# Spectral mamba stage: two of sixteen channels of the scan's feed on POOL, the skip term as one product of 512 columns

## The reference, cut to what matters

```python
dA = jnp.exp(dt[..., None] * A)
dBx = dt[..., None] * Bm[:, :, None, :] * xc[..., None]
def step(h, inp):
    dA_t, dBx_t, C_t = inp
    h = dA_t * h + dBx_t
    y = jnp.einsum('bds,bs->bd', h, C_t)
    return (h, y)
...
y = ys.transpose(1, 0, 2) + xc * D
y = y * jax.nn.silu(z)
return y @ out_w.T
```

## Time and profile before

| | us |
|---|---|
| median of 3 runs | 7898.19 (7890.61 to 7903.71) |
| the profiled execution | 7902.44, span 7900.3 |
| spectral stage: first feed to end of last scan | 5623.05 to about 7652.7 in the span |

### The profile page before, as it was taken

The page is one execution under the profiler, slowest core; times in us unless marked ns, Lnnn a source line. Parts: engine busy times, 40 slices in busy tenths (PEclk is TensorE's granted clock), DMA queues, the critical chain, the costliest instruction groups (busy, mean ns, idle before and its releaser), DMA issues. The chain is left out here.

```text
span 7900.3 us, 122279 instructions
## 1 busy us (share of the span) xinstructions
PE 6835.9 (87%) x38266; PEld 3658.0 (46%) x38266; DVE 5843.1 (74%) x5708; ACT 4011.5 (51%) x6797; POOL 3601.8 (46%) x2430
## 2 busy tenths in 40 slices
PE   8967699999965499778999999999899999999970
PEld 7842333333244145662222222222477777777750
DVE  4652577777613385018999999999799999999975
ACT  4423366666612474015666666666455555555532
POOL 0100122222202000006777777777687787787860
PEclk9988799999977798668999999999899999999985
DMA  2252234334357333440000000000000000000016
GB/s 70 69 174 103 58 99 99 99 99 100 92 124 236 129 101 116 120 65 14 14 14 14 13 15 13 13 15 9 15 11 10 10 10 11 9 10 10 10 40 188
DMA packets 560486, 478.16 MB, mean 61 GB/s; under 512 B 181789, under 2 KB 486851, under 8 KB 551771
## 3 DMA queue, kind: packets, MB, share of 16 engines
q1 hardware_dynamic: 560155, 473.52, 21.9%
HBM read 306.97 MB, written 163.76 MB: 60 GB/s over the span
## 5 line engine op out<-in xcount | busy, mean ns | idle before, releaser
L2657 POOL TENSOR_TENSOR spe_hc<-spe_hs,spe_cu 128x1024 f32<-128x1024 f32 x552 | 1291.3, 2359 | 312.0 <-DVE spe_hs L2854 312.0
L2253 POOL TENSOR_TENSOR spa_hc<-spa_hs,spa_cr 128x966 f32<-128x966 f32 x592 | 1224.2, 2068 | 426.5 <-DVE spa_hs L2527 410.4
L2527 DVE TENSOR_TENSOR_SCAN spa_hs<-spa_p_d,spa_hs,spa_bx 128x483 f32<-128x483 f32 x1168 | 1359.4, 1204 | 0.0
L2854 DVE TENSOR_TENSOR_SCAN spe_hs<-spe_p_d,spe_bx 128x1024 f32<-128x1024 f32 x552 | 1233.8, 2275 | 106.3 <-ACT spe_p_d L2803 105.6
L2731 PE MATMUL spe_p_y<-spe_idt,spe_hc 128*128 128x128 f32 x8832 | 1039.7, 276 | 0.0
L2731 PEld LDWEIGHTS spe_p_y<-spe_idt,spe_hc 128*128 128x128 f32 x8832 | 1018.1, 193 | 0.0
L1048 DVE TENSOR_REDUCE attention_nm<-attention_p_s 128x2 f32<-128x640 f32 x1024 | 788.9, 812 | 259.6 <-PE attention_p_s L905 258.6
L2803 ACT ACTIVATE spe_p_d<-spe_p_d 128x896 f32<-128x896 f32 x552 | 474.1, 900 | 918.8 <-PE spe_p_d L2716 918.4
L1006 ACT ACTIVATE attention_pr<-attention_p_t 128x512 f32<-128x512 f32 x1280 | 710.6, 599 | 421.4 <-PE attention_p_t L928 288.7
L2438 ACT ACTIVATE spa_p_d<-spa_p_d,spa_av 128x483 f32<-128x483 f32 x1184 | 704.0, 634 | 410.7 <-PE spa_p_d L2310 408.5
L2310 PE MATMUL spa_p_d<-spa_du,spa_hot 32*128 32x483 f32 x2368 | 643.1, 618 | 58.4 <-DVE spa_hs L2527 49.2
(11 more groups left out here) (417 smaller groups left out, 10585.6 us busy)
## 6 DMA issues: line engine op xcount, KB each, us to landing
attention_qs<-scratch_qp SPq DMA_DIRECT2D x768, 64.0 KB, 2.8
attention_rc<-scratch_den SPq DMA_DIRECT2D x128, 256.0 KB
scratch_qp<-patch_parts SPq DMA_DIRECT2D x96, 256.0 KB, 2.0
spa_xt<-scratch_x SPq DMA_DIRECT2D x148, 121.5 KB, 2.6
front_xs<-in_x_dram SPq DMA_DIRECT2D x64, 256.0 KB, 3.0
scratch_xf<-front_out SPq DMA_DIRECT2D x128, 128.0 KB, 2.5
patch_x<-scratch_xf SPq DMA_DIRECT2D x8, 2048.0 KB, 18.7
attention_xs<-in_x_dram SPq DMA_DIRECT2D x128, 128.0 KB, 4.6
```

Of the source, the lines that this page charges most:

```text
L2253: nc.gpsimd.tensor_tensor(hc[:, k % 8:k % 8 + 2, :], hs[:, k:k + 2, :], cr2[:, s % 2, :].unsqueeze(1).broadcast_to([128, 2, NA]), ALU.mult ...
L2527: nc.vector.tensor_tensor_scan(hs[:, k, v], p_d[k % 4][:, v], bx[:, k, v], 0.0 if start else hs[:, k, NA - 1:NA], ALU.mult, ALU.add).then_ ...
L2657: nc.gpsimd.tensor_tensor(hc[:, k, :, d, :].rearrange("p s d t -> p d s t"), hs[:, k % 2, d, :, :], rows, ALU.mult)\
L2854: nc.vector.tensor_tensor_scan(hs[:, k % 2, d].rearrange("p d s t -> p (d s t)"), p_d[h][:, :], bx[:, k % 2, d].rearrange("p d s t -> p (d ...
```

## The change

POOL takes channels 14 and 15 of every feed (256 of the 2048 elements), VectorE keeps channels 0 to 13 (1792). POOL reads both its operands from SBUF, and for that ScalarE's copy takes in B as well, 384 columns instead of 256; VectorE still reads B from PSUM. Scans of half h = 1 wait for POOL's part (`bx_pool`). The skip term leaves `total(k)` and becomes one matmul of 512 columns per chunk, `skip`, between `project_z` and `total(0)`.

```diff
+    DV = DE - 2
-        cu = st.sb("cu", [128, NSUB, 2, TD])
+        bcu = st.sb("bcu", [128, NSUB, 3, TD])
+        def steps(k, d):
+            n = d.stop - d.start
+            return bcu[:, k, 2, d.start * TK:d.stop * TK].rearrange("p (d t) -> p d t", t=TK).unsqueeze(2).broadcast_to([128, n, ST, TK])
+        def rows_for(v, d):
+            return v.rearrange("p (s t) -> p s t", t=TK).unsqueeze(1).broadcast_to([128, d.stop - d.start, ST, TK])
 # POOL
+            def feed(k):
+                def run(c, s, r):
+                    pool.wait_ge(cu_copied, NSUB * c + (k + 1))
+                    after(pool, scanned[1], NSUB * c + (k - 1))
+                    d = slice(DV, DE)
+                    nc.gpsimd.tensor_tensor(bx[:, k % 2, d], steps(k, d), rows_for(bcu[:, k, 0, :], d), ALU.mult).then_inc(bx_pool, 1)
+                return run
-            stream(pool, NC, UE, HEAD, 2, (1, silu_z), (2, weigh(0, 0)), (1, step_sizes), (2, weigh(0, 1)), (2, weigh(1, 0)), (2, weigh(1, 1)),
-                   (2, weigh(2, 0)), (2, weigh(2, 1)), (0, silu_x), (2, weigh(3, 0)), (2, weigh(3, 1)))
+            stream(pool, NC, UE, HEAD, 2, (2, feed(1)), (1, silu_z), (2, weigh(0, 0)), (1, step_sizes), (2, weigh(0, 1)),
+                   (2, feed(2)), (2, weigh(1, 0)), (2, weigh(1, 1)), (2, feed(3)),
+                   (2, weigh(2, 0)), (2, weigh(2, 1)), (0, silu_x), (1, feed(0)), (2, weigh(3, 0)), (2, weigh(3, 1)))
 # TensorE
+            def skip(c, s, r):
+                pe.wait_ge(x_active, c + 1)
+                after(pe, y_ready, c)
+                nc.tensor.matmul(p_y[:, :], dg[:, :], xz[:, s, 0, :], start=True, stop=False)
             def total(k):
...
-                    if k == 0:
-                        after(pe, y_ready, c)
-                    nc.tensor.matmul(p_y[:, px], dg[:, :], xz[:, s, 0, px], start=True, stop=False)
...
-                   (2, dt_a(2, 1)), (1, b_c_u(0)), (0, project_z), (2, total(0)), (2, dt_a(3, 0)),
+                   (2, dt_a(2, 1)), (1, b_c_u(0)), (0, project_z), (2, skip), (2, total(0)), (2, dt_a(3, 0)),
 # ScalarE, copy_c_u
+                    after(act, bx_pool, NSUB * c + (k - 3))
-                    nc.scalar.activation(cu[:, k].rearrange("p q n -> p (q n)"), p_bc[k % 2][:, TD:3 * TD], ACT.Copy).then_inc(cu_copied, 1)
+                    nc.scalar.activation(bcu[:, k].rearrange("p q n -> p (q n)"), p_bc[k % 2][:, 0:3 * TD], ACT.Copy).then_inc(cu_copied, 1)
 # VectorE, feed and scan
-                    nc.vector.tensor_tensor(bx[:, k % 2], steps, rows, ALU.mult).then_inc(bx_ready, 1)
+                    d = slice(0, DV)
+                    nc.vector.tensor_tensor(bx[:, k % 2, d], steps(k, d), rows_for(p_bc[k % 2][:, 0:TD], d), ALU.mult).then_inc(bx_ready, 1)
+                    if h == 1:
+                        dve.wait_ge(bx_pool, NSUB * c + (k + 1))
```

More of the change, by code:

```diff
@@ L2591, in spectral_mamba @@
                                 "dt_done", "soft_step", "soft_ready", "dt_ready", "u_ready"))
-        (bc_done, cu_copied, bx_ready, summed, y_ready, out_done, out_copied) = (
-            st.sem(n) for n in ("bc_done", "cu_copied", "bx_ready", "summed", "y_ready", "out_done", "out_copied"))
+        (bc_done, cu_copied, bx_ready, bx_pool, summed, y_ready, out_done, out_copied) = (
+            st.sem(n) for n in ("bc_done", "cu_copied", "bx_ready", "bx_pool", "summed", "y_ready", "out_done", "out_copied"))
         dta_done, decayed, scanned, weighted = st.sem2("dta_done"), st.sem2("decayed"), st.sem2("scanned"), st.sem2("weighted")
         block = st.block()
+        def steps(k, d):
[3 more added lines that the diff above has]
+            return v.rearrange("p (s t) -> p s t", t=TK).unsqueeze(1).broadcast_to([128, d.stop - d.start, ST, TK])
         @block.sync
@@ L2655, in run @@
                     d = slice(h * DE // 2, (h + 1) * DE // 2)
-                    rows = cu[:, k, 0, :].rearrange("p (s t) -> p s t", t=TK).unsqueeze(1).broadcast_to([128, DE // 2, ST, TK])
+                    rows = rows_for(bcu[:, k, 1, :], d)
                     nc.gpsimd.tensor_tensor(hc[:, k, :, d, :].rearrange("p s d t -> p d s t"), hs[:, k % 2, d, :, :], rows, ALU.mult)\
@@ L2724, in run @@
                         pe.wait_ge(weighted[h], NSUB * c + (k + 1))
-                    if k == 0:
-                        after(pe, y_ready, c)
                     px = slice(SUB * k, SUB * k + SUB)
-                    nc.tensor.matmul(p_y[:, px], dg[:, :], xz[:, s, 0, px], start=True, stop=False)
                     for n in range(ST):
-                        mm = nc.tensor.matmul(p_y[:, px], hc[:, k, n].rearrange("p d t -> p (d t)"), idt[:, :], start=False, stop=(n == ST - 1))
+                        mm = nc.tensor.matmul(p_y[:, px], hc[:, k, n].rearrange("p d t -> p (d t)"), idt[:, :], start=False, stop=(k == NSUB - 1 and n == ST - 1))
                     mm.then_inc(summed, 1)
@@ L2840, in run @@
                     after(dve, scanned[1], NSUB * c + (k - 1))
-                    steps = cu[:, k, 1, :].rearrange("p (d t) -> p d t", t=TK).unsqueeze(2).broadcast_to([128, DE, ST, TK])
-                    rows = p_bc[k % 2][:, 0:TD].rearrange("p (s t) -> p s t", t=TK).unsqueeze(1).broadcast_to([128, DE, ST, TK])
-                    nc.vector.tensor_tensor(bx[:, k % 2], steps, rows, ALU.mult).then_inc(bx_ready, 1)
+                    d = slice(0, DV)
+                    nc.vector.tensor_tensor(bx[:, k % 2, d], steps(k, d), rows_for(p_bc[k % 2][:, 0:TD], d), ALU.mult).then_inc(bx_ready, 1)
                 return run
```

## The result

The changed kernel takes 7754.1 us (median of 4 runs, 7745.4 to 7768.5) against 7898.2: ratio 0.982, 95% interval 0.980 to 0.984. That is 144 us less, where 46.6 were predicted and where VectorE alone, had it been the only bound, could have given 76. So most of the gain came from something that no term of the sum held.

A forecast was written before the change was run, and what follows sets the result against it. VectorE sets the pace, TensorE right behind. The chunk's period going from 27.83 to 27.14 saves 47.6 us over 69 chunks; less 1 us for 13 jumps, 7898.2 - 46.6 = 7852. Range 7824 to 7884.

The forecast's parts named there:

- the part on the jumps: At the loop's 13 jumps back VectorE waits 99.6 us in 26 waits for decays; the change leaves that loss as it is.
- The feed on VectorE: 276 feeds lose 256 of 2048 elements, 0.27 us each; a feed's slot becomes 1.94 us.
- The feed on POOL: POOL's product of 256 elements takes 0.72 us (bounds 0.58 and 1.26); its work per chunk goes from 23.9 to 26.8 us.
- The rule weighed there: Skill rule against the POOL feed: keep two-input elementwise work on VectorE, GpSimd being about twice as slow; an eighth estimated at 0.56.
- Rivals three and four: POOL's feed: at 1.26 us POOL falls behind, 7871, chance 0.13; at 1.5 us POOL is the bound, 7936, 0.10 including a lock.
- a lock: VectorE and POOL contending would end on the slower side; chance 0.10 together with POOL as the bound.
- The copy and the added waits on semaphores: ScalarE's copy: 128 more columns, 0.13 us four times a chunk, covered; added waits on scans and copies taken as nothing.
- The recurrence: Start times of VectorE and TensorE stepped through one chunk: period 27.83 to 27.14, 47.6 us over 69 chunks; chance 0.52 (7843 to 7861).
- its check: The same stepping for the kernel before: dt_a(1) at 4.47, period 27.83.
- The skip product: TensorE's 512-column matmul behind the gate, 0.86 us; worth 0.13 a chunk beside the shorter feed, a little less than nothing alone.
- TensorE holds what VectorE frees: Rival: dt_a can't get below 1.47, so only skip terms removed from other sub-blocks gain, 15 us: 7883, chance 0.12.
- VectorE alone decides: Rival: the waits of 0.37 and 0.07 for decays don't come; a chunk takes 26.72, 76 us less: 7822, chance 0.13.

The follow-up runs named there:

- kernel before, moved by 100: Kernel before the change, with 100 waiting instructions added on TensorE ahead of the stage's first matmul: 7793.7 us (0.987).
- feed alone, moved by 100: Kernel before with only the feed in two parts, skip term in four pieces, the loop moved by waiting instructions ahead of it: 7760.4 us (0.982).
- changed kernel against itself moved by 70: Changed kernel with 70 more waiting instructions on TensorE ahead of the stage's first matmul: 7860.7 us (0.995).
- kernel before moved by 186: Kernel before the change, with 186 waiting instructions added on TensorE ahead of the stage's first matmul: 7848.2 us (0.993).
- run with the longer body: Kernel before, its loop moved by waiting instructions ahead of it, plus 7 in front of each sum's matmuls on TensorE (body 1759 instead of 1647): 7865.0 us (0.995).

## Why the prediction was wrong

**The step that failed** stands in the part on the jumps: "The change does nothing to the jump, so I carry that loss along." The range's lower end, 7824, went by the pace of the engines alone and had no case in which the stall goes. A sign of it was in the rows: 99.6 us in 26 waits with TensorE at a granted clock of 0.50 behind a jump, on the very engine whose instructions the change cuts. The runs put in its place: whether the loop's code is loaded again at a jump depends on how many blocks it touches, and the change moved that from eight to seven by the fitted position. In the stage this is worth 104.0 us (kernel before, moved by 100), 109.5 (feed alone, moved by 100) and 108.2 (changed kernel against itself moved by 70).

**Inside the stall** two things add up, and the traces tell them apart. In the kernel before, the sub-block behind the jump takes 14.60 us on TensorE (6529.64 to 6544.24), where 6.58 is usual. dt_a, in which it waits twice on "issue", takes 6.69 instead of 1.07; the rest takes 7.91 instead of 5.51, at 1.2 GHz (granted clock 0.50) up to 6541. The kernel before moved by 186 has only one such wait, 1.2 us on average, and there the clock doesn't fall at every jump. Two stretches behind jumps of that run, columns as in the earlier trace rows:

```profile
6406.00:6408.00 2.00, 2.00 (x6) 1.16 (x5) 2.00 (x2) 0.93 (x2) 1.23 (x1) 0.50 0.00 0
6520.00:6522.00 2.00, 2.00 (x10) 1.09 (x7) 2.00 (x2) 1.17 (x2) 0.88 (x2) 1.00 0.04 8
```

At 8 of its 13 jumps the clock stays at 1.00, and the jump costs 1.8 to 2.4 us from gate to gate. At the other 5 it falls to 0.50, and the jump costs 3.6 to 4.0. The run with the longer body shows the same two groups (4 jumps at 1.8 to 2.1, 9 at 3.4 to 4.0). In the kernel before the clock falls at all 13, which cost 6.4 to 8.5. So the load of the code comes first and costs some 2 us even by itself. The low clock comes behind it and adds some 1.8 where there is one wait.

**The feed on VectorE**: right. 2.02 us and a slot of 1.94, as worked out.

**The feed on POOL**: right. 0.73 us against 0.72; no scan waited for it, and POOL kept up, though busy for 376 of 400 us (281.82 of 300) where over 380 was named as a sign. The rule weighed there did not decide. The Trainium skill, page "GPSIMD Engine Reference", section "Engine selection", has GpSimd about twice as slow on two-input work; the traces agree (2.36 us for 1024 elements on POOL, 2.29 for 2048 on VectorE). Rivals three and four, a dear feed and POOL as the bound, fall. So does a lock: VectorE's feed spreads over 3 ns in 276 cases beside a POOL that is busy 94% of the time. But the prediction's "this trace shows no such pair" holds only for the stage that it read. In the first stage VectorE multiplies two SBUF operands while POOL works on a third (`front_gs`, line 353, and `front_mg`, line 166). Of the 256 such instructions of lines 352 to 355, 7 take 0.81 to 1.02 us instead of 0.60, and all 7 lie beside an instruction of POOL (one starts at 423.56 and takes 1.02, with POOL at work from 421.85 to 425.01). That speaks for keeping VectorE's operand in PSUM, and it was not tried otherwise.

**The copy and the added waits on semaphores**: the copy takes 0.50 us instead of 0.39, and no feed waited for it from 5650 to 7300. No price of the waits shows, and none was measured by itself.

**The recurrence**: right in its mechanism, short in size. It gave 27.14, 27.27 and 27.88 for both parts, feed alone, skip alone; measured 27.31, 27.34, 27.95. Two of its terms were mis-sized: the skip product takes 0.93 instead of 0.86, and the sum behind project_out 3.77 instead of 3.67, together 0.17, which is what is missing for both parts. The first accounts for the 0.07 by which the skip product alone was off. For the feed alone the working left out a wait: dt_a(1) at 4.47, as in its check, gives scan (1, 0) at 6.58, where VectorE is ready at 6.54. The trace has it (feed at 6452.70, scan at 6454.67, 1.97 instead of 1.94). The feed's share of the gain is 28.8 to 34.3 us in the stage (39 would follow from 27.27).

**The skip product**: too large by far. It was to be worth 0.13 a chunk beside the lighter feed, 9 us. It is worth 0.03 (27.31 against 27.34), and the two ends of the stage take that back: 1851.0 against 1851.15 us from the first gate to the last, 1885.7 against 1883.9 from the first scan to the last. Beside the full feed it costs 8.7 (1926.9 against 1918.2). All that moving it brought came from where the loop then lay.

**The rival "TensorE holds what VectorE frees"** falls: dt_a took 1.08 at 6428.89 (its next start is 6429.97), below the 1.47 that the rival holds on to. So does "VectorE alone decides": the period is 27.31 and not 26.72. That its 7822 lies nearer to the measured 7754 is luck.

## What to carry to other kernels

When a stall comes at every jump back of a hardware loop and its engine waits on nothing that the profile shows, look at the number of instruction packets before pricing an edit: here one edit halved it, and so did 100 instructions that do nothing. Price an edit on an unrolled engine by its instruction count too, both inside the loop and ahead of it. And before crediting a gain to the work that was moved, run the old work with the loop in the same place.

## What the runs showed of the hardware

- The loop's code on TensorE stays where its body touches seven blocks of 256 instructions and is loaded again at each jump where it touches eight. All kernels of this study fit, with bodies of 1603 to 1759 instructions by the count from the source and one fitted position, and the limit is a narrow one: the 1603 of the changed kernel are kept, and the 1647 of the kernel before moved by 186, which start at the same place in a block, are loaded. The load is 9 packets a jump, one more than the eight blocks: from 6000 to 7300 the five kernels that load have 98 to 102 packets, the others none. No other engine was tried. The Trainium skill, page "Runtime: NRT & Kernel Launch", section "Instruction fetch mechanics", gives TensorE room for 2048 instructions, refilled in blocks of 256, and says that a taken branch out of the current two pages forces a load. The first agrees with the runs if one of the eight blocks is filled ahead of use, which is argued and not shown. The second doesn't agree if a page is such a block: a jump back over more than six blocks needed no load in the kernels with 118 or 119 packets. The runs show packets of 16 KB; that one holds 256 instructions is taken from this section and fits the count.
- Behind such a load TensorE's granted clock can fall to 0.50: at 5 of 13 jumps where a jump has one wait for code (the kernel before moved by 186), at all 13 where it has two (the kernel before).
- Waits for an event long past are not free on TensorE: 110 such instructions, 220 waits, cost 5 us and 186 cost 14 (some 51 and 59.8 us ahead of the first scan instead of 46). By an estimate from the runs with 70 to 186, about 65 fit into the idle time, and each beyond them costs some 0.11 us.
- In one profile, that of the changed kernel, the scans of the spatial stage, which nothing touched, show a median of 1405 ns instead of 1205, with first and last start as far apart as ever (3610.8 to 5568.7). The repeat of the same kernel shows 1204. The cause is open.
